# Post-norm attention and FFN layer: LayerNorm's broadcast rows copied from PSUM to SBUF on ScalarE, and one weight load moved to ScalarE's DMA queue

## What is computed

```python
def _layernorm(x, eps=1e-5):
    m = mean(x, -1); v = var(x, -1)
    return (x - m) / sqrt(v + eps)
phi = lambda t: elu(t) + 1
q, k, v = phi(x @ Wq.T + bq), phi(x @ Wk.T + bk), x @ Wv.T + bv      # 16 heads of 64
kv  = einsum('bhtd,bhtm->bhdm', k, v)
z   = 1 / (einsum('bhtd,bhd->bht', q, k.sum(t) + 1e-6) + 1e-6)
x   = _layernorm(x + (einsum(q, kv, z) @ Wo.T + bo))
gate, up = x @ (w_gate/127).T, x @ (w_up/127).T                     # hidden 3072
x   = _layernorm(x + (silu(gate) * up) @ (w_down/127).T)
```

## Time and profile before

| what | value |
|---|---|
| time before, median of 2 runs | 5131.31 us (5130.38 to 5132.23) |
| the profiled execution's own time | 5127.94 us |
| its span, first to last instruction, slowest core (core 4) | 5126.3 us |
| spans of the 8 cores | 5108.0 to 5126.3 us |
| mean granted TensorE clock, median of die 0 and of die 1 | 0.832, 0.834 |
| PE, DVE, ACT, POOL busy (core 4) | 3741.3, 1671.0, 1226.6, 29.6 us |

### The profile page before, as it was taken

One profiled execution on the slowest core, in us unless ns is written; L12 is line 12 of the kernel. 1 busy time (PEld: TensorE's weight loads), 2 busy tenths in 40 slices (PEclk: granted clock), 3 DMA queues, 4 the chain that ended last, 5 costly groups with the idle time before them and its releaser, 6 DMA issues.

```text
span 5126.3 us, 43745 instructions; the slowest of 8 cores (5108.0 to 5126.3 us)
## 1 busy us (share of the span) xinstructions
PE 3741.3 (73%) x15248; PEld 1470.9 (29%) x15248; DVE 1671.0 (33%) x2411; ACT 1226.6 (24%) x2171; POOL 29.6 (1%) x52
## 2 busy tenths in 40 slices
PE   1576547777756765799965865799975866599993
PEld 0232113333312322344421322244431322144440
DVE  0113423233232134333332133333333133333334
ACT  2233321111122333211122243311112233311112
POOL 0000000000000000000000000000000000000000
PEclk8797768888867877899977977799986977799995
DMA  5100022222211000010102000001003000001001
GB/s 160 39 1 1 0 74 74 74 74 74 72 66 66 1 0 0 25 50 25 50 33 99 1 1 0 25 33 42 34 25 123 1 1 0 25 25 50 25 25 66
DMA packets 69676, 199.99 MB, mean 39 GB/s; under 512 B 4933, under 2 KB 4934, under 8 KB 60248
## 3 DMA queue, kind: packets, MB, share of 16 engines
q1 hardware_dynamic: 60248, 176.23, 10.1%
q10 hardware_dynamic: 9216, 20.98, 1.3%
HBM read 144.75 MB, written 52.43 MB: 38 GB/s over the span
## 4 chain that ended last, share of the span: by engine, by line
PE 60%; DVE 13%; ACT 12%; DMA 8%; issue 5%; POOL 1%; DVEq 0%; ACTq 0%; SPq 0%; POOLq 0%
PE ps L729 12%; PE ps L708 12%; PE ps L754 11%; PE ps L385 5%; PE ps L579 5%; PE ps L340 4%; DVE wstage L232 3%; DVE x L236 3%; DMA wstage_i<-wu 3%; DMA wstage_i<-wg 2%; PE ps L489 1%; ACT arena L179 1%; ACT arena L502 1%; ACT arena L544 1%; PE ps L222 1%
## 5 line engine op out<-in xcount | busy, mean ns | idle before, releaser
L708 PE MATMUL ps<-y_bf,arena 128*128 128x512 bf16 x3072 | 706.3, 388 | 136.6 <-POOL arena L677 93.6
L729 PE MATMUL ps<-y_bf,arena 128*128 128x512 bf16 x3072 | 706.6, 387 | 107.4 <-DVE arena L677 107.4
L754 PE MATMUL ps<-h_arena,arena 128*128 128x512 bf16 x3072 | 694.1, 379 | 36.3 <-DVE h_arena L740 36.3
L718 ACT ACTIVATE h_arena<-ps 128x512 bf16<-128x512 f32 x384 | 228.9, 597 | 1813.1 <-PE ps L708 1813.1
L740 DVE SCALAR_TENSOR_TENSOR h_arena<-ps,h_arena 128x512 bf16<-128x512 f32 x384 | 265.7, 692 | 1044.9 <-PE ps L729 1040.8
L766 DVE SCALAR_TENSOR_TENSOR x<-ps,x 128x512 f32<-128x512 f32 x768 | 530.7, 692 | 183.9 <-PE ps L754 94.5
L385 PE MATMUL ps<-wk_bf,arena 128*128 128x512 bf16 x1024 | 289.4, 432 | 231.0 <-ACT arena L408 180.9
L708 PEld LDWEIGHTS ps<-y_bf,arena 128*128 128x128 bf16 x3072 | 304.8, 99 | 527.3 <-issue 180.9
L729 PEld LDWEIGHTS ps<-y_bf,arena 128*128 128x128 bf16 x3072 | 304.0, 99 | 494.4 <-issue 146.4
L754 PEld LDWEIGHTS ps<-h_arena,arena 128*128 128x128 bf16 x3072 | 293.6, 98 | 421.1 <-issue 80.9
L489 PE MATMUL ps<-arena,wq_bf 128*128 128x512 bf16 x1024 | 262.0, 424 | 191.7 <-DVE arena L477 191.7
(11 more groups left out here) (74 smaller groups left out, 2463.1 us busy)
## 6 DMA issues: line engine op xcount, KB each, us to landing
x<-x SPq DMA_DIRECT2D x16, 2048.0 KB, 9.7
out<-x SPq DMA_DIRECT2D x16, 2048.0 KB, 7.1
arena<-stash_wg SPq DMA_DIRECT2D x18, 1024.0 KB, 4.8
arena<-stash_wu SPq DMA_DIRECT2D x18, 1024.0 KB, 6.4
arena<-stash_wd SPq DMA_DIRECT2D x18, 1024.0 KB, 8.6
wstage_i<-wg SPq DMA_DIRECT2D x48, 256.0 KB, 3.0
wstage_i<-wd ACTq DMA_DIRECT2D x48, 256.0 KB, 2.8
wstage_i<-wu SPq DMA_DIRECT2D x48, 256.0 KB, 2.7
```

Of the source, the lines that this page charges most:

```text
L708: e.matmul(ps[b_][:, 0:512], slots[sl_][:, 512 * kk + 128 * gg:512 * kk + 128 * (gg + 1)], y_bf[:, T * kk + t_:T * kk + t_ + 512], start=( ...
L718: e.activation(h_arena[:, 512 * gg:512 * (gg + 1)], ps[b_][:, 0:512], AF.Silu, scale=S127), inc=act)
L729: e.matmul(ps[b_][:, 0:512], slots[sl_][:, 512 * kk + 128 * gg:512 * kk + 128 * (gg + 1)], y_bf[:, T * kk + t_:T * kk + t_ + 512], start=( ...
L754: e.matmul(ps[b_][:, 0:512], slots[sl_][:, 1024 * ss + 128 * mm:1024 * ss + 128 * (mm + 1)], h_arena[:, 512 * ss:512 * (ss + 1)], start=(s ...
```

## The change

It has four parts.

1. In `emit_layernorm` ACT copies both broadcast banks from PSUM into two bf16 tiles of 512 columns, `rb_sb` and `mrb_sb`, which lie in the upper half of `h_arena` (unused outside the FFN). The multiply and the subtract on DVE read these tiles instead of the banks. DVE now waits for the second copy (`bcast_evac`) and no longer for PE. The first copy waits for the two broadcast matmuls and for the previous tile's apply.
2. The release of banks 6 and 7 for the next output projection is now `bcast_evac` on ACT, in place of the end of the apply on DVE.
3. At the start of each sequence after the first, PE waits for the end of the FFN on ACT and DVE and for the last LayerNorm 2's `bcast_evac`, in place of everything given to ACT and DVE.
4. For the sequences after the first, the load of the up weights (`wu`) from the stash is issued on ACT's queue; gate and down stay on SP's.

```diff
@@ -145,6 +145,8 @@
         z_bf = arena[0:16, 10888:11400]
         slots = [arena[:, 4096 * i:4096 * (i + 1)] for i in range(4)]
         ln_scr = [(zb[0], zb[1]), (h_arena[:, 0:512], h_arena[:, 512:1024])]
+        rb_sb = h_arena[:, 1024:1536]
+        mrb_sb = h_arena[:, 1536:2048]
         tmp32 = wstage[:, 0:512]
         ln_r = wstage[0:1, 512:1024]
         m_row = wstage[0:1, 1024:1536]
@@ -169,7 +171,7 @@
         xq_state = {}
 
         def emit_layernorm(p, t0, src_ready_dve, want_ybf, ps_lo, ps_hi,
-                           entry_pe=0):
+                           entry_pe=0, prev_apply=0):
             hist = [entry_pe, entry_pe]
             stat_done = entry_pe
             for m in range(NCH):
@@ -226,22 +228,28 @@
                 ps[ps_hi][:, 0:512], ones1f[:, :], ln_r[0:1, 0:512],
                 start=True, stop=True), inc=pe)
             bc = pe.n
-            p.wait("vector", pe, bc)
+            p.wait("scalar", pe, bc)
+            p.wait("scalar", dve, prev_apply)
+            p.op("scalar", lambda e: e.copy(rb_sb[:, :], ps[ps_lo][:, 0:512]))
+            p.op("scalar", lambda e: e.copy(mrb_sb[:, :], ps[ps_hi][:, 0:512]),
+                 inc=act)
+            bcast_evac = act.n
+            p.wait("vector", act, bcast_evac)
             for m in range(NCH):
                 p.wait("vector", dve)
                 p.op("vector", lambda e, mm=m, t_=t0: e.tensor_mul(
                     tmp32[:, :], x32[:, T * mm + t_:T * mm + t_ + 512],
-                    ps[ps_lo][:, 0:512]), inc=dve)
+                    rb_sb[:, :]), inc=dve)
                 p.wait("vector", dve)
                 p.op("vector", lambda e, mm=m, t_=t0: e.tensor_sub(
                     x32[:, T * mm + t_:T * mm + t_ + 512], tmp32[:, :],
-                    ps[ps_hi][:, 0:512]), inc=dve)
+                    mrb_sb[:, :]), inc=dve)
                 if want_ybf:
                     p.wait("scalar", dve)
                     p.op("scalar", lambda e, mm=m, t_=t0: e.copy(
                         y_bf[:, T * mm + t_:T * mm + t_ + 512],
                         x32[:, T * mm + t_:T * mm + t_ + 512]), inc=act)
-            return stats_read, dve.n, bc
+            return stats_read, dve.n, bcast_evac
 
         p = Prog()
         p.dma("sync", scst, bq_sb[:], bq_d[:])
@@ -306,8 +314,9 @@
         for b in range(BPC):
             xq_loaded = xq_state[b]
             if b > 0:
-                p.wait("tensor", act)
-                p.wait("tensor", dve)
+                p.wait("tensor", act, prev_guard["p3_act"])
+                p.wait("tensor", dve, prev_guard["ffn_done"])
+                p.wait("tensor", act, prev_guard["ln2_evac"])
                 p.wait("vector", pe)
                 for _ss in slot_sem:
                     p.wait("scalar", _ss)
@@ -468,6 +477,7 @@
             a_mult = [0] * NCH
             stats_free = kv_ready
             bcast_free = 0
+            ln1_apply = 0
             q_mm_last = kv_done[TCH - 1]
             for tile in range(NTILE):
                 t0 = 512 * tile
@@ -570,8 +580,7 @@
                 for m in range(NCH):
                     bank = 6 + m % 2
                     p.wait("tensor", dve, o_free[m % 2])
-                    p.wait("tensor", act, stats_free)
-                    p.wait("tensor", dve, bcast_free)
+                    p.wait("tensor", act, max(stats_free, bcast_free))
                     for k in range(NCH):
                         p.wait("tensor", act, wcast["wo"][k])
                         p.wait("tensor", dve, a_mult[k])
@@ -591,7 +600,8 @@
                              ALU.add, ALU.add), inc=dve)
                     o_free[m % 2] = dve.n
                 o_done = dve.n
-                stats_free, bcast_free, _ = emit_layernorm(p, t0, o_done, True, 6, 7)
+                stats_free, ln1_apply, bcast_free = emit_layernorm(
+                    p, t0, o_done, True, 6, 7, prev_apply=ln1_apply)
 
             if stage == 1:
                 p.flush(nc)
@@ -632,9 +642,10 @@
                     dest = slots[slot_i]
                     if b > 0:
                         ssem = slot_sem[slot_i]
-                        p.wait("sync", *stash_val[(wname, hc)])
-                        p.wait("sync", pe, slot_war[slot_i])
-                        p.dma("sync", ssem, dest[:, :], stash[wname][hc])
+                        ldq = "scalar" if wname == "wu" else "sync"
+                        p.wait(ldq, *stash_val[(wname, hc)])
+                        p.wait(ldq, pe, slot_war[slot_i])
+                        p.dma(ldq, ssem, dest[:, :], stash[wname][hc])
                         rdy = (ssem, ssem.n)
                         for kk in range(NCH):
                             slot_ready_k[slot_i][kk] = rdy
@@ -773,18 +784,24 @@
                 if hc + 1 < NHC:
                     emit_ffn_loads(hc + 1)
             ffn_done = dve.n
+            prev_guard = {"p3_act": act.n, "ffn_done": ffn_done, "ln2_evac": 0}
 
             for _ss in slot_sem:
                 p.wait("scalar", _ss)
             p.wait("scalar", pe)
             prev_apply = ffn_done
             prev_bc = 0
+            ln2_apply = 0
             next_x = []
             for tile in range(NTILE):
                 t0 = 512 * tile
-                _, ap_done, prev_bc = emit_layernorm(
-                    p, t0, prev_apply, False, 6, 7, entry_pe=prev_bc)
+                _, ap_done, _bev = emit_layernorm(
+                    p, t0, prev_apply, False, 6, 7, entry_pe=prev_bc,
+                    prev_apply=ln2_apply)
+                ln2_apply = ap_done
+                prev_bc = pe.n
                 prev_apply = ap_done
+                prev_guard["ln2_evac"] = _bev
                 p.wait("sync", dve, ap_done)
                 p.dma("sync", so,
                       out_d[b].rearrange("(k p) t -> p k t", p=128)
```

## The result

The changed kernel is slower by 0.7%: the ratio to the kernel before is 1.007, with a 95% interval of 1.0048 to 1.0092. Its fastest execution took 5168.8 us, beside 5130.1 us for the kernel before in the same session. That is 38.7 us more, where the prediction had 37.4 more and 5169 us. In some executions of most kernels here one die or both had a lower granted clock (down to 0.73 in the mean, in place of 0.83), and these are left out of all ratios and times compared, though not of the changed kernel's median over all its runs, 5275.8 us.

A forecast was written before the change was run, and what follows sets the result against it. PE carries 60% of the chain of waits, and all 32 LayerNorms lie on the path. Copies 38.4, guard -1.0, other terms 0 give +37.4 us on 5127.94, plus 3.4 to the runs' median: 5169 us; 8-in-10 range 5136 to 5190.

The forecast's parts named there:

- All 32 norms on the path: Every LayerNorm on a core is waited for, so latency between broadcast and apply is paid 32 times.
- The two copies at 1.20 us: ACT's copies between broadcast and apply delay DVE's multiply by 1.20 us per LayerNorm, 38.4 us in all.
- The biased pair of the earlier trace: Two similar ACT reads with a bias operand, 1.43 us; taken as the copies' other end, 45.8 us.
- One sign: In the changed profile, ACT's wait before the LayerNorm 2 statistics (L179) was to grow by 1.2 us.
- The apply from SBUF at 0: LayerNorm's 512 DVE multiplies and subtracts keep about 687 ns with SBUF operands; -3.6 to +3.1 us, taken as 0.
- Both rivals that paid the copies back: SBUF operands shorten the DVE apply: by 51 us, giving 5118 us (4%), or by 33 us, giving 5136 us (6%).
- The earlier release of banks 6 and 7: nothing: The output projection gains 0, since it comes behind the Q projection, whose cast follows the apply.
- PE's guard at -1 us: At a new sequence's start clearing matmuls run during the apply: -1 us for all three, between -1.2 and 0.
- The up load at 0: In the FFN, the load on ACT's queue stays hidden, with 2.3 us left at an FFN's start: 0.
- The sum: Whole kernel: 38.4 + 0 + 0 - 1.0 + 0 = +37.4 us, predicting 5169 us, 0.7% slower.

The follow-up runs named there:

- the mirror image: Kernel before, no copies; the multiply waits only for the first broadcast matmuls, the subtract for the second: 0.9949, 5100.5 us at best beside 5124.1.
- The copies alone: Kernel before plus only the two ACT copies, waited for by DVE but read by nobody: 1.0075, fastest 5164.9 us beside 5126.6.
- the overlapped kernels: LayerNorm 2 statistics beside the previous apply: changed kernel waiting for the FFN's end instead, 0.9802; kernel before with two bank pairs and split waits, 0.9681.

## Why the prediction was right, step by step

- **All 32 norms on the path.** Right. DVE's wait has 32 entries before and after and grew by 1.18 us each; the mirror image took the same kind of latency out of 32 places and won 23.6 us of 25.
- **The two copies at 1.20 us, from the L406, L408, L415 pattern.** Right: 1.18 by the sum of the waits, 37.8 us of the 38.4 forecast. In the tile shown the pair takes 1.24 us from the first copy's start, 0.04 more than the neighbour, but the first copy starts a little sooner behind the broadcast than the multiply did, and 1.16 is left. The biased pair of the earlier trace rows was the wrong neighbour, as supposed. The copies alone cost 38.3 us. One sign came otherwise than written: ACT's wait ahead of the statistics did not grow by 1.2 us, since the copies now stand inside it (17.9 before, 5.1 and 12.9 now).
- **The apply from SBUF at 0.** Right to within 2.4 us: 512 instructions at 692 ns in place of 687 (177.2 + 177.1 us now, 176.0 + 175.9 before). They still start 0.80 us apart (1576.96, 1577.76), so the gap between them wasn't owed to the PSUM operand. Both rivals that paid the copies back fall with it. The table of the Trainium skill, "VectorE: DVE Perf Modes", "The TRN2 errata", would have made each instruction 65 ns shorter (an estimate from its cycles); the trace shows it 5 ns longer, and the measurement decides.
- **The earlier release of banks 6 and 7: nothing.** No wait of the output projection (L579 before, L588 now) shows in either trace. It wasn't tested by itself; the copies alone, which keep the old release, cost as much as the whole change.
- **PE's guard at -1 us.** Right in size: 0.27 us in 3 places, 0.8 us.
- **The up load at 0.** Right, with more room than I counted: 4.5 us left at an FFN's start in place of 2.3, since the load landed in 4.8 us where 6.4 was taken.
- **The sum.** 37.8 + 2.4 - 0.8 = 39.4 us from the traces; 38.7 measured between the fastest runs. That the forecast of 37.4 came so near is in part luck: the interval of the ratio allows 25 to 47 us. It is the waits and durations at the 32 places that carry the account, and not the total.

What stays open is small. The times can't tell the last 2 to 3 us of the sum apart, and the moved load is known to be free to 0.3% only.

## What to carry to other kernels

In this kernel a copy out of PSUM paid only where something that was waiting for the bank really started earlier. Elsewhere, look for the wait that the free bank releases, and move that one too; here the copies cost 0.7% with the old wait kept and gained 2% with it gone, and a second pair of banks did the same job with no copy. In a serial chain that repeats, price each hop by the nearest pair of rows (first read's start to the released engine's start) times the number of places, and look first for parts of the chain that can signal by themselves.

## What the runs showed of the hardware

A VectorE tensor_tensor of 128x512 in f32 takes 687 ns with its second operand in PSUM and 692 ns with it in SBUF, whether that is bf16 or f32. The two ACT copies of 128x512 f32 from PSUM take 585 and 592 ns into bf16, and 586 and 592 into f32. ACT reading and squaring one tile of x, PE summing ACT's copies of it and DVE applying the norm to the tile before, all at the same time, did not slow the apply: in the overlapped kernels it stayed at 692 (with copies) and 687 to 688 ns (without). At the start of a sequence, behind a LayerNorm 2, PE's granted clock is at its lower level, and it reaches the upper one at a time that scatters from one sequence to the next, with no link to the guard that shows. In the kernel before, at the second sequence, the first 8 K matmuls take 3.59 us at a granted clock of 0.50 (1.2 GHz), the next 8 take 2.72 at 0.69, and the first 8 V matmuls 1.90 at 1.00 (2.4 GHz). In the changed kernel the first 8 take 3.19 us at 0.58, and the next 8 take 1.90 at 1.00.
